# Attention: softmax rows turned in 32x32 blocks by VectorE, and P x V for two heads in one product over array pieces

## The reference

```python
x = x + 0.5 * ffn(layernorm(x))           # 1024 -> 1024, bias, LoRA
# attention, on layernorm(x):
q = rmsnorm(x @ wq_a.T, q_a_ln_w) @ wq_b.T          # latent 256 -> 32 heads x 128
ckv, k_pe = split(x @ wkv_a.T)                      # 64 + 64
kv = rmsnorm(ckv, kv_a_ln_w) @ wkv_b.T              # 64 -> 32 heads x (64 + 128)
q_pe, k_pe = rope(...), rope(...)
scores = (q_full @ k_full.T) * softmax_scale        # causal
attn = softmax(scores, axis=-1)
out = (attn @ v) ; x = x + out @ wo.T
x = x + 0.5 * ffn(layernorm(x))
```

## Time and profile before

| | |
|---|---|
| median of 3 runs | 2160.96 us (2159.16 to 2163.87) |
| the profiled execution | 2158.76 us, span of its instructions 2156.9 us |
| attention, first fold to the first load of the output phase | 351.7 to 1574.3 us |
| a pair of heads in the loop | 74.86 us |
| TensorE busy in span | 96%, in the attention 100% |
| VectorE, ScalarE, GpSimd busy in the loop | 45.4, 47.2, 61.3 of 74.86 us |

### The profile page before, as it was taken

The page is one execution under the profiler, slowest core; times in us unless marked ns, Lnnn a source line. Parts: engine busy times, 40 slices in busy tenths (PEclk is TensorE's granted clock), DMA queues, the critical chain, the costliest instruction groups (busy, mean ns, idle before and its releaser), DMA issues. The chain is left out here.

```text
span 2156.9 us, 36532 instructions
## 1 busy us (share of the span) xinstructions
PE 2065.4 (96%) x11120; PEld 1624.2 (75%) x11120; DVE 1113.0 (52%) x2589; ACT 952.9 (44%) x2151; POOL 1113.3 (52%) x833
## 2 busy tenths in 40 slices
PE   6999797999999999999999999999969999997999
PEld 4778696777777777777777777777748888875887
DVE  5555284656665665665666666556642111114553
ACT  2111274666666666666666666666631101003110
POOL 2222102888888888888888888888600000004321
PEclk9999898999999999999999999999989999998999
DMA  6432421121122112112211211111173232304421
GB/s 230 165 137 88 129 98 61 52 66 35 55 65 62 43 55 62 39 52 63 65 40 55 65 40 56 60 61 35 40 244 117 88 107 86 109 30 177 154 90 67
DMA packets 96697, 180.25 MB, mean 84 GB/s; under 512 B 16448, under 2 KB 53440, under 8 KB 94592
## 3 DMA queue, kind: packets, MB, share of 16 engines
q1 hardware_dynamic: 96640, 179.51, 26.2%
HBM read 120.49 MB, written 58.98 MB: 83 GB/s over the span
## 5 line engine op out<-in xcount | busy, mean ns | idle before, releaser
L907 PE MATMUL psS<-keyT,q 128*128 128x256 f32 (+2 forms) x2304 | 513.5, 358 | 4.8 <-POOL q L1124 4.3
L907 PEld LDWEIGHTS psS<-keyT,q 128*128 128x128 f32 x2304 | 382.4, 189 | 87.9 <-DVE negmax L1054 27.0
L993 ACT ACTIVATE prob<-prob,negmax 128x128 f32<-128x128 f32 (+7 forms) x512 | 393.1, 771 | 74.9 <-DVE negmax L1054 74.8
L1054 DVE CUSTOM_DVE_ANT_0 prob<-psS,mask 128x128 f32<-128x128 f32 (+7 forms) x512 | 381.9, 755 | 78.3 <-PE psS L907 55.1
L1000 ACT ACTIVATE pT<-psT 128x512 f32<-128x512 f32 (+2 forms) x384 | 201.8, 525 | 350.3 <-PE psT L918 348.6
L1085 DVE COPY pT<-psT 128x256 f32<-128x256 f32 (+3 forms) x384 | 196.9, 513 | 307.0 <-PE psT L918 305.9
L918 PE MATMUL psT<-ident,prob 128*128 128x128 f32 x2304 | 338.1, 274 | 1.6 <-ACT prob L993 1.1
L413 PE MATMUL f_psy<-f_weff,f_xT 128*128 128x512 f32 x1344 | 313.5, 392 | 0.0
L1282 PE MATMUL o_psy<-o_w,o_o 128*128 128x512 f32 x1344 | 304.8, 389 | 0.0
L918 PEld LDWEIGHTS psT<-ident,prob 128*128 128x128 f32 x2304 | 268.6, 140 | 33.0 <-issue 11.4
L1282 PEld LDWEIGHTS o_psy<-o_w,o_o 128*128 128x128 f32 x1344 | 252.3, 188 | 52.4
(11 more groups left out here) (101 smaller groups left out, 2009.2 us busy)
## 6 DMA issues: line engine op xcount, KB each, us to landing
wo<-in_wo SPq DMA_DIRECT2D x16, 1024.0 KB, 5.2
o_scale<-row_scales SPq DMA_DIRECT2D x64, 256.0 KB, 3.4
oT<-o_sum SPq DMA_DIRECT2D x128, 128.0 KB, 2.3
o_in<-oT SPq DMA_DIRECT2D x32, 512.0 KB, 5.3
f_xt<-in_x SPq DMA_DIRECT2D x16, 512.0 KB, 4.1
f_w_in<-in_w SPq DMA_DIRECT2D x16, 512.0 KB, 6.6
w_sum<-f_w_in SPq DMA_DIRECT2D x16, 512.0 KB, 5.1
x<-f_xo SPq DMA_DIRECT2D x16, 512.0 KB, 2.8
```

Of the source, the lines that this page charges most:

```text
L907: ins = nc.tensor.matmul(psS[:, li % 2, shift + x0:shift + x1], q[:, s % 2, a, t * P:(t + 1) * P], k.keyT[:, m, b * S + x0:b * S + x1], st ...
L993: nc.scalar.activation(row, row, ACT.Exp, bias=negmax[:, li % 8:li % 8 + 1], scale=-1.0, accum_out=rowsum[:, col:col + 1]).then_inc(exped, 1)
L1054: nc.vector.tensor_tensor_reduce(out=prob[:, li % 4, 0:(t + 1) * P], in0=place(s, t), in1=k.mask[:, S - (t + 1) * P:S], scale=-1.0, scalar ...
```

## The change

A step is now one batch of a pair, both heads together: two steps per pair, 32 in all, 16 score tiles per step, tile n being query tile n // 2 of head n % 2.

- PE's transposes, `psT`, and the copies L1000 and L1085 are gone. VectorE transposes each 32x32 block of a row of `prob` in place of its block, SBUF to SBUF, one instruction per tile (`transposes`), from `prob` (now 8 slots) to `pT` (per head, 8 x 1024).
- `values`: one per key block kt, behind the last transpose of the step. A 128x128 block turned only within 32x32 leaves query rows of block i in partition group i. So a product has 32 rows (the keys of one 32-block), 64 columns of weights and up to 512 moving columns (both heads), and goes to bank i of `psV`, which now has four banks: 16 fp32 products per kt, four row groups times two column halves, 128 per step.
- `val` is laid out so that each group of 32 partitions has every key block. For it the latents phase stores the values to DRAM (16 stores), and the attention loads them in 32 DMAs.
- ScalarE copies the upper half of each bank into a part of `cosT`/`sinT` that is free (`evict_values`), VectorE adds the lower in two instructions of 64x256 (`join_values`), GpSimd scales both heads at once (`scale_values`, 128 partitions).
- Queries: ScalarE copies three times (plain, and the two rope quarters crossed over), GpSimd does three operations, not four, and the rounding goes from VectorE to ScalarE (`query_hi`). `qf`, `swapped`, `o_raw`, `o_scale` lie in parts of `pT` that causality leaves free.
- Q, F and W use the banks of `psV`.

```diff
@@ latents_phase, SP @@
                 if has(2):
                     sp.wait_ge(f.normed, n + 1)
                     sp.dma_start(f.xt[:, j, :], src_d[bass.ds((n + 2) * P, P), :]).then_inc(f.x_in[j], 16)
-            steady(sp, step, NT, 2, start=0)
+                if has(-1):
+                    sp.wait_ge(latent, n)
+                    sp.dma_start(v_d[bass.ds((n - 1) * P, P), :], lat[:, (j + 1) % 2, QR:QR + KVR]).then_inc(k.v_stored[(j + 1) % 2], 16)
+            steady(sp, step, NT, 2, 1, start=0)
...
@@ the order @@
-PE_STEP = ("S7-1 S0+0 T5-1 Q0+1 T6-1 T7-1 V0-1 S1+0 T8-1 S2+0 T9-1 Q1+1 T10-1 T11-1 S3+0 S4+0 T0+0 T1+0 F0+0 W0+0 "
-           "S5+0 T2+0 S6+0 V1-1 T3+0 T4+0")
...
+PE_STEP = ("F0-1 S9-1 F1-1 Q0+0 S10-1 S11-1 Q1+0 S12-1 S13-1 W0-1 S14-1 S15-1 Q2+0 S0+0 S1+0 S2+0 Q3+0 S3+0 S4+0 S5+0 "
+           "S6+0 V0-1 V1-1 V2-1 V3-1 S7+0 V4-1 V5-1 V6-1 V7-1 S8+0")
+ACT_STEP = ("E9-1 E10-1 Q1+0 E11-1 E12-1 H0+0 E13-1 W0-1 H1+0 E14-1 E15-1 Q2+0 E0+0 Q3+0 E1+0 E2+0 H2+0 E3+0 E4+0 E5+0 "
+            "H3+0 E6+0 E7+0 O0-1 O1-1 O2-1 F0+0 F1+0 O3-1 E8+0 Q0+1")
+DVE_STEP = ("T0+0 M5+0 M6+0 T1+0 T2+0 T3+0 T4+0 M7+0 T5+0 T6+0 T7+0 O0-1 M8+0 O1-1 F0+0 M9+0 F1+0 T8+0 O2-1 M10+0 "
+            "M11+0 T9+0 T10+0 M12+0 M13+0 T11+0 T12+0 M14+0 M15+0 O3-1 M0+1 T13+0 M1+1 M2+1 T14+0 M3+1 M4+1 T15+0 R0+0 "
+            "R1+0")
+POOL_STEP = ("B2+0 B3+0 A0+1 A1+1 B0+1 B1+1 P0-1 P1-1 A2+1 A3+1")
+SP_STEP = ("L0+0 X1+0 Z0+1 X0+1 K0+1 Y0+0 Y1+0")
...
@@ PE @@
-            def transposes(it, s, g):
...
-                for kt in range(blocks):
-                    ins = nc.tensor.transpose(psT[:, (NG * s + g) % 2, kt * P:(kt + 1) * P],
-                                              prob[:, (QT * s + t) % 4, (k0 + kt) * P:(k0 + kt + 1) * P], k.ident[:])
-                ins.then_inc(turned, 1)
...
+            def values(it, kt, s):
+
+                step, b = it * 2 + s, s % 2
+                if kt == 0:
+                    pe.wait_ge(turned, step * TILES + TILES)
...
+                for a in range(BLOCKS // 2):
+                    for half in range(2):
+                        for i in range(BLOCKS):
+                            rows, block = slice(32 * i, 32 * i + 32), BLOCKS // 2 * half + a
+                            x = kt * P + 32 * block
+                            out = psV[KVR * half:KVR * half + KVR, i, :].rearrange("p (e t r) -> p e t r", e=2, r=32)
+                            ins = nc.tensor.matmul(out[:, :, kt:QT, :], val[rows, b, block, kt, :], pT[rows, :, kt:QT, x:x + 32],
+                                                   start=(kt == 0 and a == 0), stop=(kt == QT - 1 and a == BLOCKS // 2 - 1))
                 ins.then_inc(valued, 1)
...
@@ ACT @@
-                nc.scalar.activation(qf[:, ch, :], psM[:, :], ACT.Copy).then_inc(m_free, 1)
...
+                nc.scalar.activation(qf[:, n % 2, :], psV[:, n, :], ACT.Copy)
+                nc.scalar.activation(swapped[64:96, n % 2, :], psV[96:128, n, :], ACT.Copy)
+                nc.scalar.activation(swapped[96:128, n % 2, :], psV[64:96, n, :], ACT.Copy).then_inc(q_copied, 1)
...
+                act.wait_ge(valued, step * QT + QT)
+                if later(step, 1):
+                    act.wait_ge(evicted, step * 4 + bank - 3)
+                nc.scalar.activation(upper(bank), psV[KVR:P, bank, :], ACT.Copy).then_inc(copied, 1)
...
@@ DVE @@
+            def transposes(it, n, s):
+
+                step, t, width = it * 2 + s, n // 2, (n // 2 + 1) * P
+                dve.wait_ge(exped, step * TILES + n + 1)
                 if later(step, 1):
+                    dve.wait_ge(valued, (step - 1) * QT + t + 1)
+                nc.vector.transpose(pT[:, n % 2, t, 0:width], prob[:, n % RING, 0:width]).then_inc(turned, 1)
...
+            def join_values(it, bank, s):
+
+                step = it * 2 + s
+                dve.wait_ge(copied, step * 4 + bank + 1)
                 if later(step, 1):
+                    for ch in range(2):
+                        dve.wait_ge(o_stored[ch], step * 16)
+                for e in range(2):
+                    x = slice(e * 32 * QT, (e + 1) * 32 * QT)
+                    halves = [y.rearrange("p (h t r) -> p h t r", h=2, r=32) for y in (psV[0:KVR, bank, x], upper(bank)[:, x])]
+                    ins = nc.vector.tensor_tensor(by_block(o_raw, bank)[KVR * e:KVR * e + KVR], halves[0], halves[1], ALU.add)
+                ins.then_inc(evicted, 1)
```

More of the change, by code:

```diff
@@ L494, in _, with latents_phase @@
             ffn_steps(dve, step)
-def latents_phase(nc, k, src_d, args, ahead):
+def latents_phase(nc, k, src_d, args, ahead, v_d):
     wa_d, lnw_d, cos_d, sin_d = args
@@ new lines, in attention_phase, with spare, place, column @@
+        block = stack.enter_context(nc.Block())
+        def spare(e, t0, t1):
+            return pT[:, e, t0:t1, CHUNK:S]
+        qf, swapped = spare(0, 0, 2), spare(0, 2, 4)
+        o_raw, o_scale = spare(1, 0, 2), spare(1, 2, 4)
+        def place(n):
+            x = P if n // 2 == 4 else 0
+            return psS[:, n % 2, x:x + (n // 2 + 1) * P]
+        def column(n, s):
+            return 2 * QT * (s % 2) + n // 8 * QT + n % 2 * 4 + n // 2 % 4
+        def folds(it, n, s):
+            return 2 * (it + (s + 1) // 2) + n + 1
@@ L815, in _, with upper, by_block @@
+        def upper(bank):
+            return (cosT, sinT)[bank // 2][0:KVR, bank % 2 * BANK:(bank % 2 + 1) * BANK]
+        def by_block(tile, i):
+            return tile.rearrange("p h (t a r) -> p h t a r", a=BLOCKS, r=32)[:, :, :, i, :]
         @block.sync
@@ L895, in scores, with queries @@
-            def scores(it, s, t):
-                li, b = QT * s + t, (s // 2) % 2
-                if later(it * TILES + li - 1, 1):
-                    pe.wait_ge(maxed, it * TILES + li - 1)
+                ins.then_inc(f_done, 1)
+            def queries(it, n, s):
+                ch, e, b = n // 2, n % 2, s % 2
+                pe.wait_ge(f_split, folds(it, e, s - s % 2 - 1))
+                for i, (a, m) in enumerate(PASSES):
+                    for t in range(QRT):
+                        ins = nc.tensor.matmul(psV[:, n, :], wq[:, a, e, t, :], k.qnT[:, m, t, b * S + ch * CHUNK:b * S + (ch + 1) * CHUNK],
+                                               start=(i == 0 and t == 0), stop=(i == 2 and t == QRT - 1))
+                ins.then_inc(q_done, 1)
@@ new lines, in query_hi, with exponentials @@
+            def query_hi(it, n, s):
+                act.wait_ge(roped, (it * 2 + s) * 4 + n + 1)
+                nc.scalar.activation(q[:, n % 2, HI, n // 2 * CHUNK:(n // 2 + 1) * CHUNK], qf[:, n % 2, :], ACT.Copy).then_inc(q_hi, 1)
+            def exponentials(it, n, s):
+                step, width = it * 2 + s, (n // 2 + 1) * P
+                act.wait_ge(maxed, step * TILES + n + 1)
+                if n % 8 == 0 and later(step, 2):
+                    act.wait_ge(recip, step * 2 - 3 + n // 8)
+                row = prob[:, n % RING, 0:width]
+                nc.scalar.activation(row, row, ACT.Exp, bias=negmax[:, n % 8:n % 8 + 1], scale=-1.0,
+                                     accum_out=rowsum[:, column(n, s):column(n, s) + 1]).then_inc(exped, 1)
@@ L1053, in maxima @@
+            def maxima(it, n, s):
+                li, width = (it * 2 + s) * TILES + n, (n // 2 + 1) * P
+                dve.wait_ge(scored, li + 1)
+                if later(li, RING):
+                    dve.wait_ge(turned, li - RING + 1)
                 dve.sem_inc(allowed, 1)
-                nc.vector.tensor_tensor_reduce(out=prob[:, li % 4, 0:(t + 1) * P], in0=place(s, t), in1=k.mask[:, S - (t + 1) * P:S],
+                nc.vector.tensor_tensor_reduce(out=prob[:, n % RING, 0:width], in0=place(n), in1=k.mask[:, S - width:S],
@@ L1136, in body @@
             def body(r):
[L1137 to L1140 removed]
+                job, n, s = list(Round(0).jobs(POOL_STEP))[-1]
+                before = None if r.first else (job, n, s - 2)
+                for job, n, s in r.jobs(POOL_STEP):
                     if before:
[L1143 removed]
+                        finished(r.it, *before)
```

484 lines of the change are left out of this document (211 added, 273 removed).

## The result

The changed kernel takes **2088.1 us** (median of 4 runs, 2086.6 to 2089.9), the kernel before 2161.6 us: a ratio of 0.966 (95% interval 0.964 to 0.968). So the gain is 73 us where 149 were forecast. The time lies within the range, but the likeliest case was too low by 76 us. The profiled execution has a span of 2085.4 us. One run among all those of this document, of experiment 7, took 2660 us at a granted clock of 0.65 from end to end and is left out of its median.

A forecast was written before the change was run, and what follows sets the result against it. PE bounds the attention now; after the change PE's 29.9 and VectorE's 30.0 us floors plus 2 us of hand-overs make 32.0 us per step. Sum: 2158.8 - 168 + 19 + 2 = 2012 us, range 1945 to 2200.

The forecast's parts named there:

- the likeliest case: Whole kernel: 2012 us, from 32.0 us per attention step and a loss in the latents.
- PE's sum: TensorE per attention step: 21.4 us that stay plus 8.5 us of products, eight pieces at once, 29.9 us.
- VectorE's durations: VectorE per attention step: maxima 10.8, transposes 11.2, joins 2.6, 1/rowsum and fold 1.1 us, together 25.7 us.
- The latents: Latents phase: `x` load waits behind a store, tiles 7.0 in place of 5.37 us apart, 19 us lost.
- the hand-over term: Attention step: PE standing, S1's wait for GpSimd and the first join's wait for stores, 2 us; 34.5 if counted twice.
- The two floors that lean on each other: Attention step: PE's 29.9 us and VectorE's loop of 30.0 us, in a fixed order, set its length.
- the ring: Experiments' finding: products, ScalarE's copies, joins, any folds, Q0, three copies, eight GpSimd operations (10.9 us), S1, last transposes, products.
- Products bound by issue or by row groups (1): Attention's products: 256 weight-load and matmul pairs per step cost more; 2250, 2284 or 2607 us; chance 14%.
- Two cycles per column (2): VectorE's transpose takes two cycles per column, 9 us more per step, 2300 us; chance 4%.
- Engines mesh worse (3): Attention loop: each hand-over can cost a microsecond, 34.5 to 36.5 us per step, 2095 to 2160 us; chance 14%.
- No loss in the latents and 30 us per step (4): Better case for latents and attention: 1930 us; chance 4%.
- Wrong: a granted clock under 1.00 in the loop: Sign in the profile of the attention loop, where PE had no holes so far, that would show the prediction wrong.

The follow-up runs named there:

- experiment 7: Kernel with the three edits plus, per step, one VectorE instruction (2012.4 us), three TensorE matmuls (2011.0 us) or one ScalarE copy (2015.5 us).
- kernel with the three edits: Changed kernel with output stores first in SyncE's order, two buffers for the turned 1/rowsum, and latents value stores three tiles behind: 2011.5 us.
- experiment 5: Changed kernel with the latents' value stores three tiles behind and the folded weights' first load ahead of the last stores: 2066.8 us.
- Experiments 1 to 3: Changed kernel, SyncE order: `wo` load behind output stores (2033.2 us); stores also ahead of `turn_scales` (2032.5); only half of `wo` behind stores (2053.6).
- experiments 7 and 8: Kernel with the three edits: work added on VectorE, TensorE, ScalarE (2012.4, 2011.0, 2015.5 us) or GpSimd (2026.5); GpSimd started earlier (1993.2); low parts moved to VectorE (2070.0).
- second kernel: Changed kernel with the output stores ahead of `turn_scales` and the `wo` load in SyncE's order: 2032.5 us.
- fastest kernel: Kernel with the three edits, GpSimd's rotation starting behind the first of ScalarE's three query copies, not the third: 1993.2 us.

## Why the prediction was right or wrong, point by point

- **PE's sum: right.** Products at 8.4 us (8.5 forecast), PE busy 29.7 us in a step without folds and 31.3 in one with them, 30.5 on average, where 29.9 were forecast.
- **VectorE's durations: right.** A tile's transpose 757 ns on average, 0.78 forecast with its overlap; 1.04 ns per column. Two joins of a bank take 0.85 us, not 0.66, 0.8 us more per step. The stretch from the first join to the end of the last transpose is 20.9 us in a step without folds (kernel with the three edits; 19.7 forecast, with the folds). VectorE is busy 26.5 and 27.3 us per step, 25.7 forecast.
- **The latents: right.** 21.7 us late against 21, tiles 7.1 to 7.5 us apart against 7.0, and experiment 5 gives them back. VectorE waits there for the DMA of `l_xt`, 37.3 us in 14 waits.
- **The step that failed** is the hand-over term: "the stores of the output are queued on SP behind `turn_scales` and, every other step, behind the load of `wo`, and the first join waits for them (0.5)". The mechanism was named, its size was not worked out: it was 3.8 us in 15 steps (57.3 us), 1.8 on average per step, and taking it away was worth 58 us between the profiled executions where the term had 16. I had counted the issues in the queue, and not that a 256 KB store behind 1 MB on the same engines lands after 6.3 us. Experiments 1 to 3 show it: without the load ahead the wait is gone, with half of it it halves. That the time still lies in the range owes much to luck: the upper bound let each hand-over count twice, and this one counted 3.6 times.
- **The two floors that lean on each other: near in number, wrong in reason.** Without that wait a step takes 32.34 us on average; 31.5 were forecast without its term. But the step is set by the ring, of which the prediction had only "S1 waits for the second head's B1 on GpSimd, which has seven operations ahead of it (0.5 to 1)" as a delay on top of a floor. That GpSimd and ScalarE "are not the bound" was read from their busy sums. The probes of experiments 7 and 8 show it otherwise: VectorE and TensorE took 0.6 us for nearly nothing, and GpSimd did not.
- **Rivals.** Products bound by issue or by row groups (1): did not happen, eight pieces at once, 33 ns per pair. The Trainium skill, "TensorE: Matmul & The Clock Gate", section "Wait — 56ns, not 53.3ns?", gives 62 ns for a matmul that the sequencer's program decodes; the trace shows nothing of it here. Two cycles per column (2): did not happen. Engines mesh worse (3), 34.5 to 36.5 us per step: nearest, with 34.3, and with the right kind of cause, a hand-over of several microseconds. No loss in the latents and 30 us per step (4): the first only with the edit of experiment 5, and the shortest steps of any run average 31.9 us, at 1993. The forecast's lower end of 1945 doesn't follow from its bounds: 30 us per step and no loss in the latents make 2012 - 64 - 19 = 1929, the case of rival 4.
- **"Wrong: a granted clock under 1.00 in the loop"**: happened, 0.95 in the window of a step with the `wo` load, mostly in the steps with the wait, and worth some 14 us of its own (below).

## What to carry to other kernels

When a change lets an engine wait for a store that it never waited for before, price the store behind everything ahead of it on its queue, in bytes and not in issues: here moving one load behind two stores was worth 55 us of 2088. A sum of busy times per engine doesn't show a ring that goes through all of them once per step; follow it with one step's timelines from release to release, and tell its engines from the idle ones by adding half a microsecond to each. An edit that shortens the ring pays only down to the next floor, so add the same half microsecond again after it.

## What the hardware showed unexpectedly

The clock. Before the change TensorE had no holes in the loop and a granted clock of 1.00. After it, PE stands for 2.34 us at 885.4 in the step with the `wo` load, and 1 us after its work begins again at 887.8 the granted clock is at 0.50, the lower level of 1.2 GHz, for 3.4 us. Three windows in a row:

```profile
885.40:888.70 3.30, 0.96 (x5) 0.81 (x5) 1.80 (x5) 0.23 (x2) 0.00 (x0) 1.00 0.16 59
888.74:892.14 3.40, 3.40 (x11) 2.74 (x11) 3.00 (x8) 2.95 (x6) 0.27 (x1) 0.50 0.21 61
892.20:895.60 3.40, 3.40 (x19) 2.95 (x18) 3.10 (x6) 2.69 (x6) 3.24 (x3) 1.00 0.00 0
```

This happened in 12 of the 15 steps with the wait and in two of the others, and with the wait gone (second kernel) in one place of the loop. What it costs can be read from steps that differ in nothing else that the profile shows. Of the changed kernel here are two steps without folds, whose joins both wait 3.4 us for the stores, and of the kernel with the three edits two steps with folds:

```profile
1078.00:1111.70 33.70, 29.79 (x361) 21.19 (x361) 26.32 (x60) 25.07 (x53) 23.10 (x19) 1.00 0.23 72
1010.10:1044.50 34.40, 30.96 (x361) 22.50 (x361) 26.46 (x61) 24.97 (x53) 23.11 (x19) 0.95 0.22 71
...
1181.10:1214.60 33.50, 31.35 (x370) 22.27 (x370) 27.50 (x65) 25.88 (x57) 23.25 (x19) 1.00 0.14 48
1245.70:1280.00 34.30, 32.48 (x364) 23.43 (x364) 27.70 (x65) 25.85 (x57) 23.26 (x19) 0.95 0.15 48
```

So 3.4 us at the lower level cost 0.7 to 0.8 us here, and 1.2 us in the fastest kernel (34.0 against 32.8). In the changed kernel the three waiting steps at a clock of 1.00 are longer than the 31.2 us of the second kernel by their wait less 0.85 us; the twelve others are longer than that by 13 us in all (two have 6.8 us at the lower level), the two steps with folds by 1.5. That makes some 14 us, which went together with the waits. What brings the fall is not settled: in the loop of the kernel with the three edits it came once, in the last step shown, after work that was the same as in its neighbours. No run held the clock apart from the waits. The other surprises are those told above: VectorE's instruction with two SBUF inputs that ends 0.55 us after GpSimd's, and 256 pairs of weight load and product at 33 ns each.
